# Two of four bisection counts as sign sums on ScalarE, with another order of the work, in a cross-attention and two-expert FFN kernel

## What is computed

```python
h = layernorm(x)                                     # (8, 512, 256)
Q, K, V = h @ WQ + bQ, ctx @ WK + bK, ctx @ WV + bV  # 16 heads of 16
x = x + (softmax(Q K^T * mask) / 4 @ V) @ Wp + bp

def perturb(w):            # scale 0.8; W1: 256x1024, W2: 1024x256, b1, b2
    a, n = abs(w), w.size
    k = max(1, int(n * 0.05))
    bottom, top = sort(a)[k - 1], sort(a)[n - k]
    return w + 0.8 * w * where(a >= top, -1, where(a <= bottom, 1, 0))

h = layernorm(x)
probs = softmax((layernorm(h) * gamma + beta) @ Wr + br)     # 8 experts
y0 = gelu(h @ W1 + b1) @ W2 + b2
y1 = the same with the perturbed W1, b1, W2, b2
out = x + probs[0] * y0 + sum(probs[1:]) * y1
```

## Time and profile before

| | us |
|---|---|
| median of 3 runs | 717.68 |
| lowest, highest | 712.82, 719.94 |
| the profiled execution | 718.19 |
| its span in the profile | 716.3 |
| PE, DVE, ACT, POOL busy in it | 660.0, 475.7, 394.6, 240.9 |

### The profile page before, as it was taken

The page is one execution under the profiler, slowest core; times in us unless marked ns, Lnnn a source line. Parts: engine busy times, 40 slices in busy tenths (PEclk is TensorE's granted clock), DMA queues, the critical chain, the costliest instruction groups (busy, mean ns, idle before and its releaser), DMA issues.

```text
span 716.3 us, 15490 instructions
## 1 busy us (share of the span) xinstructions
PE 660.0 (92%) x5555; PEld 602.0 (84%) x5555; DVE 475.7 (66%) x1219; ACT 394.6 (55%) x504; POOL 240.9 (34%) x266
## 2 busy tenths in 40 slices
PE   3658979999999589999999999997999999999996
PEld 2548978998998489999999999896888988889885
DVE  3668796788787778778778678456965434544352
ACT  4344657658656346856856855545644354434442
POOL 2342444474575436466456346333000000000000
PEclk9867669999999889999999999699899999999998
DMA  6977412614705602542541441230101132212321
GB/s 190 193 165 136 99 67 76 121 38 136 122 31 145 117 2 89 120 85 91 115 84 80 92 92 43 78 118 33 56 1 33 56 88 88 64 38 74 88 59 29
DMA packets 131251, 61.51 MB, mean 86 GB/s; under 512 B 104570, under 2 KB 121988, under 8 KB 131204
## 3 DMA queue, kind: packets, MB, share of 16 engines
q1 hardware_dynamic: 121108, 58.33, 33.4%
q10 hardware_dynamic: 10096, 2.56, 2.0%
HBM read 34.64 MB, written 22.03 MB: 79 GB/s over the span
## 4 chain that ended last, share of the span: by engine, by line
PE 82%; DVE 8%; issue 2%; DMA 2%; ACT 2%; SPq 1%; POOL 1%; DVEq 0%; ACTq 0%; POOLq 0%
PE ps_l L358 10%; PE ps_l L359 8%; PE ps_l L360 8%; PE ps_y L358 8%; PE ps_m L688 8%; PE ps_y L359 8%; PE ps_y L360 8%; PE ps_m L774 5%; PE ps_s L656 4%; PE ps_s L676 3%; PE ps_s L358 2%; PE ps_s L360 2%; PE ps_s L359 2%; PE ps_m L728 2%; DVE ind L1527 1%
## 5 line engine op out<-in xcount | busy, mean ns | idle before, releaser
L1044 ACT ACTIVATE region_b<-ps_l,bias 128x512 f32<-128x512 f32 x128 | 88.0, 688 | 148.9 <-PE ps_l L360 146.5
L1782 DVE TENSOR_TENSOR region_c_lo<-region_b,region_c_hi 128x512 fp32r<-128x512 f32 x72 | 49.7, 692 | 98.1 <-ACT region_c_hi L1047 94.9
L1312 POOL TENSOR_TENSOR region_c_lo<-region_b,region_c_hi 128x512 fp32r<-128x512 f32 x56 | 75.2, 1349 | 92.1 <-ACT region_c_hi L1047 92.0
L1047 ACT ACTIVATE region_c_hi<-ps_l,bias 128x512 fp32r<-128x512 f32 x128 | 87.3, 682 | 10.0 <-PE ps_y L360 10.0
L1286 POOL TENSOR_TENSOR region_a<-region_a,mx 128x1024 f32<-128x1024 f32 x32 | 63.6, 1986 | 64.0 <-DVE mx L1430 64.0
L358 PE MATMUL ps_y<-w_hi,region_c_hi 128*128 128x256 f32 x256 | 76.5, 299 | 0.0
L1527 DVE TENSOR_SCALAR ind<-key,cand 128x2048 bf16<-128x2048 uint16 x93 | 73.7, 834 | 0.2
L360 PE MATMUL ps_y<-w_hi,region_c_lo 128*128 128x256 f32 x256 | 73.6, 288 | 0.0
L359 PE MATMUL ps_y<-w_lo,region_c_hi 128*128 128x256 f32 x256 | 73.5, 287 | 0.0
L688 PE MATMUL ps_m<-vbd,region_a 128*128 128x34 f32 x512 | 67.6, 290 | 3.4 <-DVE on L1440 2.8
L688 PEld LDWEIGHTS ps_m<-vbd,region_a 128*128 128x128 f32 x512 | 65.6, 207 | 4.1 <-issue 3.5
(11 more groups left out here) (224 smaller groups left out, 1706.0 us busy)
## 6 DMA issues: line engine op xcount, KB each, us to landing
qs<-q_scr SPq DMA_DIRECT2D x16, 512.0 KB, 6.1
xa<-in_x SPq DMA_DIRECT2D x8, 512.0 KB, 5.0
q_scr<-qn_lo SPq DMA_DIRECT2D x16, 256.0 KB, 5.4
x<-in_x SPq DMA_DIRECT2D x32, 128.0 KB, 4.0
region_b<-x SPq DMA_DIRECT2D x8, 512.0 KB, 3.0
out_x<-acc SPq DMA_DIRECT2D x32, 128.0 KB, 2.4
acc_scr<-acc SPq DMA_DIRECT2D x7, 514.0 KB, 5.1
acc<-acc_scr SPq DMA_DIRECT2D x7, 514.0 KB, 3.3
```

Source lines behind the costliest of these rows:

```text
L1044: act.activation(g[:, f % 4, :], ps_l[:, f % 2, :], ACT.Gelu_apprx_tanh, bias=bias[:, e, f:f + 1]).then_inc(s["gelu"].handle, 1)
L1047: act.activation(gs[0][:, f % 4, :], ps_l[:, f % 2, :], ACT.Gelu_apprx_tanh, bias=bias[:, e, f:f + 1]).then_inc(s["g_hi"].handle, 1)
L1312: pool.tensor_tensor(gs[1][:, f % 4, :], g[:, f % 4, :], gs[0][:, f % 4, :].bitcast(F32), ALU.subtract).then_inc(s["g_lo"].handle, 1)
L1782: dve.tensor_tensor(gs[1][:, f % 4, :], g[:, f % 4, :], gs[0][:, f % 4, :].bitcast(F32), ALU.subtract).then_inc(s["g_lo"].handle, 1)
```

## The change

Search 2 goes the way of search 3: ACT sums its signs too, and DVE's compare and PE's 16 matmuls for it are gone, in all 31 steps. The bodies have another order on PE, ACT, POOL and DVE; SP's order stays. The set-up keeps its order, with two sums where one stood, and now finishes the count of step 6, whose `total` opens body 1. Where the code waits for six masked scores before `turn_x2` it waits for four, and the scores wait for `x2T_ready` at chunk 2, not 3.

```diff
-    ind_ready = sig("ind_ready", 3)
-    ind_counted = sig("ind_counted", 3)
-    signs_summed = sig("signs_summed")
+    ind_ready = sig("ind_ready", 2)
+    ind_counted = sig("ind_counted", 2)
+    signs_summed = sig("signs_summed", 2)
...
         for t in range(NT):
             router(0, t)
+        for s in range(2):
+            count(6, s)
...
             turn_probs(i, 0, last)
             h(0)
-            count(p, 0)
+            h(1)
+            total(p)
             if not last:
                 turn_queries_input(i + 1)
-            count(p, 1)
-            count(p, 2)
-            h(1)
-            total(p)
             values(i, 0)
+            h(2)
             turn_probs(i, 1, last)
-            h(2)
             c(0, 0)
+            h(3)
+            c(0, 1)
             if not last:
                 queries(i + 1)
-            c(0, 1)
             values(i, 1)
+            h(4)
+            t(0)
             turn_probs(i, 2, last)
-            c(0, 2)
-            h(3)
-            t(0)
+            o(0)
             turn_probs(i, 3, last)
             values(i, 2)
-            o(0)
...
+            o(1)
             values(i, 3)
-            o(1)
+            h(5)
             turn_output(i)
...
+            c(1, 0)
+            c(1, 1)
+            o(2)
             t(1)
-            h(5)
             project(i, 0)
             project(i, 1)
             h(6)
             s(0, 0)
+            c(2, 0)
             s(0, 1)
-            o(2)
-            c(2, 0)
-            o(3)
+            h(7)
             s(1, 0)
             s(1, 1)
-            h(7)
+            c(2, 1)
+            o(3)
+            turn_x2(i)
...
-        def sum_signs(k, rnd):
+        def sum_signs(k, rnd, which=(2, 3)):
 
             wait(act, cand_step, k - 1)
-            act.activation(ind[3][:], key[:, key_of[rnd][3], :], ACT.Sign, bias=cand[:, 3:4], scale=-1.0,
-                           accum_out=signs[:]).then_inc(signs_summed.handle, 1)
+            for s in which:
+                act.activation(ind[s][:], key[:, key_of[rnd][s], :], ACT.Sign, bias=cand[:, s:s + 1], scale=-1.0,
+                               accum_out=signs[:, s - 2:s - 1]).then_inc(signs_summed.handle, 1)
...
-            dve.tensor_copy(cnt[:, 0:3], ps_m[:, 1, 0:3]).then_inc(cnt_ready.handle, 1)
+            dve.tensor_copy(cnt[:, 0:2], ps_m[:, 1, 0:2]).then_inc(cnt_ready.handle, 1)
             wait(dve, signs_summed, k)
-            dve.tensor_scalar(cnt[:, 3:4], signs[:], 0.5, float(WN // 2), ALU.mult, ALU.add).then_inc(cnt_ready.handle, 1)
+            dve.tensor_scalar(cnt[:, 2:4], signs[:], 0.5, float(WN // 2), ALU.mult, ALU.add).then_inc(cnt_ready.handle, 1)
...
-            top_scores(i, 3)
-            counts(p)
-            if not last:
-                low_queries_input(i + 1)
             decide(p)
             if turn:
                 end_first_round()
-            cmp(0, 0, 1)
+            if not last:
+                low_queries_input(i + 1)
+            cmp(0, 0)
+            top_scores(i, 3)
+            cmp(0, 1)
             if not isinstance(i, int) or i + 2 < B:
                 wait(dve, x_in, i + 2)
                 stats(0, i + 2, xa)
-            cmp(0, 2)
             normalise_output(i, 0)
+            if turn:
+                lower_keys(0)
+            cnts(0)
             if not last:
                 low_queries(i + 1)
-            if turn:
-                lower_keys(0)
-            probabilities(i - 1)
             normalise_output(i, 1)
...
-            masks(1)
+            mask_one(1, 0)
+            mask_one(1, 1, False)
+            cnts(2)
+            mask_top(1)
+            dec(2)
             mask_one(2, 0)
             mask_one(2, 1, False)
-            cnts(2)
-            dec(2)
+            low_x2(i)
+            cmp(3, 0, 1)
             mask_top(2)
             mask_one(3, 0)
-            cmp(3, 0)
             mask_one(3, 1, False)
-            low_x2(i)
+            probabilities(i - 1)
+            base(0, i - 1)
+            cnts(3)
+            logits(i)
             if last:
                 mark_weights(0, 1)
                 perturb_weights(0, 1)
             mix(0, i - 1)
-            logits(i)
-            cmp(3, 1, 2)
```

More of the change, by code:

```diff
@@ L185, in build_program @@
     cnt = sb("cnt", [P, NS])
-    signs = sb("signs", [P, 1])
+    signs = sb("signs", [P, 2])
     fail = sb("fail", [P, NS])
@@ L650, in scores @@
             else:
-                if j == 3 and not first:
+                if j == 2 and not first:
                     wait(pe, x2T_ready, b - 1)
@@ L717, in turn_x2 @@
             if to is ps_s and (not isinstance(b, int) or b + 1 < B):
-                wait(pe, s_masked, b + 1, 6)
+                wait(pe, s_masked, b + 1, 4)
             for c in range(DC):
@@ L840, in _ @@
         scores(0, 3, 1)
-        for s in range(3):
+        for s in range(2):
             count(1, s)
@@ L1192, in body @@
             turned(i, 2)
+            if not turn:
+                cmp(1, 2)
             turned(i, 3)
+            more_gelu(3)
             if not turn:
-                cmp(1)
-            more_gelu(2)
-            more_gelu(3)
+                cmp(1, 3)
             high_output(i)
+            more_gelu(4)
             if turn:
@@ L1211, in body @@
             more_gelu(6)
+            cmp(2, 3)
             more_gelu(7)
+            copy_x2(i)
+            router_exp(i - 1)
+            high_x2(i)
             if not last:
                 probs(i + 1, 0)
-            copy_x2(i)
-            high_x2(i)
+            cmp(3, 2)
             if not last:
                 probs(i + 1, 1)
-            cmp(3)
+            cmp(3, 3)
         def last_expert():
@@ L1346, in body @@
             shift(i, 3)
+            low(0)
             if more:
                 rsqrt(0, i + 2)
+            low(1)
+            if more:
+                normalise(0, i + 2, xa, 0, 1)
             bias_residual(i, 0)
             bias_residual(i, 1)
[L1351 to L1354, removed]
             bias_residual(i, 2)
             low(2)
[L1357 to L1360, removed]
             if more:
                 normalise(0, i + 2, xa, 2, 3)
+            low(3)
+            bias_residual(i, 3)
             low(4)
@@ L1366, in body @@
             if not last:
[L1367 removed]
+                normalise(1, i, x2, 0, 1, 2, 3)
+            low(6)
+            if not last:
                 shift(i + 1, 0)
[L1369 to L1372 removed]
                 shift(i + 1, 1)
             router_rsqrt(i)
+            low(7)
         def last_expert():
@@ L1737, in _ @@
         decide(5)
+        logits(0)
         compares(6, 0)
-        logits(0)
+        counts(6)
         steps = [0]
@@ L1855, in body @@
             normalise_output(i, 2)
-            base(0, i - 1)
+            normalise_output(i, 3)
             if turn:
```

64 lines of the change are left out of this document (22 added, 42 removed).

## The result

The changed kernel took 729.0 us (median of 4 runs, 727.5 to 729.7) beside 717.3 for the kernel before: a ratio of 1.018, interval 1.014 to 1.022. The forecast was 714.5 and a range up to 724.0; what came is, in its mechanism, the rival "the holes take the clock", priced at 726.5 and given 0.18.

A forecast was written before the change was run, and what follows sets the result against it. PE was taken as the bound, busy throughout a body; five bodies -5.5, turn body -2.0, set-up +5.7, last body and expert -1.8 sum to -3.6 us from 718.19, so 714.6, set at 714.5; range 706.5 to 724.

The forecast's parts named there:

- the holes take the clock: Rival: xa lands at 12.9, holes of 1.7 us, each followed by 3.1 us at half clock; 726.5 us, chance 0.18.
- part (a): At values(i,1), bodies 2 to 5: PE waits for a result behind the late xa load; 0.5 us, ends 0 and 1.7.
- Counts off PE: Each body: four counts of search 2 leave PE, 0.40 us each, 53.32 - 1.6 = 51.7 us.
- (b): At project: ACT copy and DVE subtraction take 2.6 us beside 2.45 of other work, a hole of 0.15 us.
- (c): At turn_x2: residual, statistics, rsqrt and normalised tiles need 7.2 to 7.3 us against 7.2, a hole of 0.1 us.
- ACT's load: Each body: four more sums of 2.10 us make ACT 45.1 us busy of 51.7; no wait of PE for ACT counted.
- the third rival: ACT becomes the bound: waits at ACT's margins bring bodies back to 53.3 us, total 720 us; chance 0.07.
- drain: ACT table loads: the skill page adds about 1.38 us each, giving 50.6 of 51.7; the forecast said the trace disagrees.
- The turn body: Body that rewrites the keys: laid out at 64.6 us against 66.6, -2.0, ends -4 and +1.
- Set-up: Before body 1: second sums and the new count of step 6 delay the first turn_probs; +5.7 us, ends +3.5 and +8.
- Last body and expert: Final stage: new order helps the first half, 2.5 us added for the clock; -1.8 us, ends -4.3 and +1.
- No holes, warm clock: Rival: xa lands in 4.8 us, the hole closes, clock falls don't come, last body keeps full clock; 707.5 us, chance 0.27.

The follow-up runs named there:

- e1: Changed kernel with normalise_output(i,0) moved on DVE ahead of the wait for xa and its statistics; 713.9 us, ratio 0.997 to the kernel before.
- e3: Changed kernel with three counts and one sum in set-up's search steps 0 to 6, bodies as changed; 725.8 us, ratio 1.017 to the kernel before.
- e7: Kernel before, with SP issuing two of the four residual loads ahead of the load of xa and two behind it; 718.1 us, ratio 1.003.
- e8: Kernel before with the second sum alone, its compare and count removed, order otherwise as before; 728.0 us, ratio 1.020.
- e11: Kernel before with one unused DVE reduction ahead of normalise_output(i,0) in bodies 1, 2, 4, 5 and 6; 719.3 us, ratio 1.003.
- e4: Changed kernel's order, but three counts and one sum everywhere, set-up included; 742.0 us, ratio 1.040 to the kernel before.

## Why the prediction was wrong, point by point

**The step that failed** is the sum of part (a): "With 5.3 ... xa is there at 11.5 and the hole is 0.3; a tenth or two go to the semaphores: I take 0.5, ends 0 and 1.7". The mechanism stood in the text with its place, its order and its bodies; measured, the hole was 1.62 to 2.06 us. Two terms were short, both the same way. In body 2 the mix ended 0.9 later and the load took 0.5 more (5.8 for 5.3), with 1.8 for SP between them as laid out; in body 4 the load took 1.3 more. The second half is what a hole of that size does: the sum has no term for the clock behind it. It was forecast only in the rival ("each followed by such a fall of 3.1 us at half clock"), which had the condition right (xa at 12.9) and the fall too short, 6.8 us. In the place of 0.5 us a body stand 1.9 + 3.4. That the rival's 726.5 is near 729.0 is in part luck: its falls were half as long as those that came, and it kept the -1.8 of the last stage, where -5.0 came by the clock of the kernel before.

**Why the mix was late** is argued, not shown. DVE and POOL in body 1 of the changed kernel:
```profile
159.15 1.90 POOL L1286 TENSOR_TENSOR region_a<-region_a,mx 128x1024 f32<-128x1024 f32 x1
162.83 1.72 POOL L1312 TENSOR_TENSOR region_c_lo<-region_b,region_c_hi 128x512 fp32r<-128x512 f32 x1
```
```profile
159.72 1.36 DVE L1561 TENSOR_SCALAR half<-half 128x2 f32<-128x2 f32 x1
163.33 2.43 DVE L1524 TENSOR_SCALAR ind<-key,cand 128x2048 bf16<-128x2048 uint16 x2
```
A step on two numbers, elsewhere as short as 0.17 us, took 1.36 and ended 0.03 after POOL's instruction; two compares, elsewhere 1.42, took 2.43. Both lie in DVE's unbroken row ahead of the last mask, which ended 1.2 later than laid out. I had given each instruction its undisturbed duration. The Trainium skill ("SBUF — State Buffer", SBUF: two separate sides) says that GpSimd shares a pair of ports with VectorE's instructions in a two-port mode or with two SBUF inputs, and that whichever starts first has the pair for its whole instruction. By that, ends 0.03 apart are no accident, and the trace agrees. No run moved POOL's work away, so this cause stands untested.

**Counts off PE:** 1.6 us a body forecast. The undisturbed bodies take 52.4 to 52.6 against 51.95 laid out and 53.32 before, so 0.7 to 0.9 came. **The small holes** (b) and (c): 0.22 and 0.43 at `project` in bodies 2 and 1, none at `turn_x2`. **ACT's load:** 43.98 busy of 45.1 forecast, and no wait of PE for it in a loop body: the third rival did not come, and no drain was seen either (the load of a table began at 170.99 and the Gelu behind it at 172.29, 1.30 later).

**The turn body:** -0.7 for -2.0; it has the 1.78 us hole with its fall, and 1.92 for `qn_lo`; without the hole (e1) it takes 64.25, laid out 64.6. **Set-up:** +8.0 for +5.7, at the upper end. The direction and count 6 were right (2.8 here, laid out 2.9); the sums were too small: the router's matmuls began 5.1 us later (107.00 for 101.93) and not 2.7, and with one sum (e3) only 0.8. **Last body and expert:** -5.0 for -1.8, and the reason does not hold. The sum set the new last body, with 2.5 us for the clock, beside an old one whose trace had lost 6.8. With both at clock 1.00 the new one is 3.2 us longer (46.87 for 43.64, above). From the start of the last body to the end, the other kernels of the new order took 266.5 to 270.7 us, and the others of the old order (e7, e8, e11) 263.8 to 266.4; the 272.0 before was the exception. So the direction came right by luck, by the clock of one execution.

**The rivals.** "No holes, warm clock" is what e1 shows of the bodies (clock 1.00 in 2, 4, 5 and 6), but at 713.9 us and not 707.5: set-up took 7.7 more for 5.7, and in the last body the clock fell. So the change carried a gain of 0.7 to 2.5 us in each loop body (e1's beside those of the earlier trace rows; 0.7 to 0.9 where those had no fall of the clock), and lost it behind one wait. The parts alone carry none: the order alone costs 4%, the sums alone 2%.

**What stays open.** Why the clock falls in the old order without a hole. Over the traces of all kernels of the old order here (one execution each, bodies 1, 2, 4, 5 and 6), it fell for 3.4 us in 10 of the 16 bodies in which PE never waited over 0.7 us; in the new order with two counts in none of 29 that had no wait over 0.5 us at `values(i,1)`. Neither the order nor the counts explain this alone: with the new order and three counts (e4) it fell twice with no wait over 0.2 us in the 13 us before, and with the old order and two counts (e8) in three of five bodies. In the new order a hole at `values(i,1)` of 1.5 to 2.5 us was followed by a fall in 9 of 10 cases, of 1.0 to 1.2 in 1 of 6. Of the two holes of that length in the old order one had a fall behind it.

## What to carry to other kernels

When one engine works a list in order, look at every instruction that waits for a transfer and ask what stands behind it and who wants that; here a result that PE needed stood behind statistics that nobody needed yet, and moving it ahead gave 15 us. A margin that is laid out from undisturbed durations to within a microsecond is no margin: the terms that were short here (DVE beside POOL, a load behind its stores) all lengthened, so such a hole belongs at its upper end, with what the clock does behind it added. Compare two layouts at the same clock: a stage that one trace shows at half clock is no measure for a new order. Test an order and an operation apart and together: here each alone loses, and both together, with the one wait mended, come out level with the kernel before or up to 1% under it.

## What the runs showed of the hardware that I had not expected

- PE's clock falls after the hole, not in it: 1.1 us into the busy stretch behind a hole of 1.62 us, for 6.8 us; in the other loop bodies of the new order 0 to 2.1 us behind the hole, for 3.4 or 6.8 us.
- The load of 512 KB took 3.5 to 3.8 us (bodies 2 to 5) ahead of two stores from the same queue, 4.2 to 5.1 between them, 5.4 to 6.6 behind them.
- An instruction of 0.17 us on DVE took 1.36 us beside one of 1.90 on POOL, and `sind` of 0.18 took 1.89 beside one of 2.34.
